# Records of q and k: computed in turned layout and assembled through HBM, in a two-layer attention kernel

## The chip, the cores and the metric

One core of one Trainium2 chip. The metric is the device time of one execution in microseconds; three executions of the kernel before are shown, and the smaller the better. Names used below: PE is TensorE (the matmul engine), DVE is VectorE, ACT is ScalarE, POOL is GpSimd, SP is SyncE, which here only issues transfers (DMAs). SBUF is the on-chip memory of 128 partitions, PSUM the eight accumulation banks that matmuls write, HBM the memory off the core.

## The reference

Two batches of 1024 tokens, 512 wide. Four steps in a row, each added to its input:

```python
x = x + attn_a(layernorm(x), w_qkv_a, w_o_a)   # rope on even/odd pairs, theta 10000
x = x + ffn(layernorm(x), kernel, scale)       # scale * (x @ (2*kernel - 1))
x = x + attn_b(layernorm(x), w_qkv_b, w_o_b)   # rope on halves, base 500000
x = x + ffn(layernorm(x), kernel, scale)
# attention: 32 query heads, 8 key/value heads, 16 wide, causal
q, k, v = split(x @ w_qkv, [512, 128, 128])
q, k = rope(q), rope(k)
scores = q @ k.T / 4 + causal mask;  out = softmax(scores) @ v;  return out @ w_o
```

## The kernel before

It runs four rounds (two batches times two layers), all unrolled inside a loop over `b` and `l`. Each engine has its own queue and works through it in the order in which it is written; semaphores order the engines among each other.

**Stage A** of a round makes q, k and v for 8 tiles of 128 tokens, in slots: in slot n tile n is projected while older tiles are worked on. `PE_SLOT`, `ACT_SLOT` and `DVE_SLOT` list what an engine does in a slot, and `LAG` says for which tile. For a tile, `qkv` (L483) multiplies with the tokens as the stationary operand and 512 or 256 columns of the weights moving, in three products (high times high, high times low, low times high) for precision. ACT copies the result out (`QC`, L747 to L749), DVE and POOL rotate it with tables (`rope_cos` L942, `rope_sin` L1111, `rope` L950). Then each 16-wide head is split in three bf16 parts h, m and l: `part_h` (ACT, L759 and L760), `rest` (POOL, L1122 and L1123), `part_m` (ACT, L766 and L767), `part_l` (DVE, L957 and L959). They are written side by side as a **record** of 7 slots of 16 values (h h h m m l l for q, in another order for k), so that one matmul of depth 112 gives a score of nearly fp32 precision; three more rows hold the negated row maximum of each query. The record is token by token, so PE turns it, head by head, with a matmul against a bf16 identity (`turn_rec`, L532: five batches of eight heads for each tile), and ACT and DVE copy the turned batches from PSUM into `qT` and `kT` (L740, L935).

In the same slots PE and DVE work off the 22 **units** of key/value group 0 (L549 and L551; `unit`, L974): a unit computes scores of a query tile against all its keys and takes their maximum. Units of query tiles 0 to 3 are numbers 0 to 5, those of tiles 4 to 7 are numbers 6 to 21, 16 of them.

**Groups**: then, for each of the 8 key/value groups, scores (L571), exp (ACT, L793), masks (POOL), times v (L589), and the maxima of the next group. The first matmul of L571 in a round is where stage A ends. The `Tail` projects with w_o, adds the FFN and normalises for the next round; ACT and POOL split the next `w_qkv` there (L727, L1098).

SP's queue in a round: the maxima's rows of group 0 (`put_nm`, L409), w_o, 15 more rows, the next w_qkv, and in the last layer of a batch stores and loads of x.

Of the kernel before, what the change touches and what calls it, by code (L numbers as in the profile page):

```python
# [13 lines left out]
P = 128  # L14
# [27 lines left out]
SLOTS = 8  # L42
MAXROW = (SLOTS - 1) * HD
DEPTH = MAXROW + 3
RECS = 3

AHEAD = TILES // 2  # L50
# [9 lines left out]
TURNS = TILES + len(CD_TILES)  # L60
# [136 lines left out]
LAG = {"TX": -1, "Q": 0, "R": 3, "U": 4, "HI": -1, "LO": -1, "QC": 0, "COS": 1, "ROPE": 1, "PH": 1, "PM": 2, "PL": 2,  # L197
       "RC": 3, "ST": -4, "RS": -3, "AP": -2}
# [3 lines left out]
SLOTS_A = range(-4, TILES + 4)  # L202
SLOT_NM = TILES + 2


def slot_work(text, n):

    out = []
    for what, *arg in words(text):
        t = n - LAG[what]  # L210
        if what in ("ST", "RS", "AP"):
            if t % 2 == 0 and 1 <= t // 2 < PAIRS:
                out.append((what, arg, t // 2))
        elif 0 <= t < TILES and (what != "U" or arg[0] < len(units_of(t))):
            out.append((what, arg, t))
    return out


def qkv_bank(t):

    return 2 if t == 1 else 0


def unit_pair(g_is_first, n):


    return n % 2 if not g_is_first or UNITS[n][0] > QT_PER_CHUNK else 1
# [13 lines left out]
def build(nc, x, w_qkv, w_o, w_ffn, scale, cos, sin, eye, tri, out):  # L241
    with ExitStack() as ctx:
# [40 lines left out]
        k_rec = sb("k_rec", [P, RECS, KV, SLOTS, HD], BF16)  # L283
# [175 lines left out]
        def _(pe):  # L459
# [27 lines left out]
            def round_(b, l, r):  # L487
# [7 lines left out]
                def qkv(t, k, part):  # L495

                    T = r * TILES + t
                    if part == 0:
# [5 lines left out]
                        if t == 0:  # L504
                            pe.wait_ge(wq_hi_done, r * KC + KC)
# [742 lines left out]
```

## Time and profile before

| what | us |
|---|---|
| median of 3 executions (1553.36 to 1553.91) | 1553.46 |
| span of the profiled execution, first to last instruction | 1552.2 |
| so what lies around the span, against the median | 1.3 |
| PE busy | 1439.5 (93%) |
| DVE busy | 1132.0 (73%) |
| ACT busy | 998.2 (64%) |
| POOL busy | 413.6 (27%) |
| stage A of the four rounds, from the first matmul of L483 to the first of L571 | 87.05, 83.80, 83.90, 83.33 |

The page gives busy time as a share of the whole span; a stage is read with the view that gives busy times for a stretch. A time such as "x8" in a row covers eight instructions together.

### The profile page before, as it was taken

How to read it: one execution, taken by the hardware profiler on the slowest of the kernel's cores; microseconds unless marked ns; L12 is line 12 of the kernel's file. 1: busy time of each engine (PE TensorE's matmuls, PEld its weight loads, DVE VectorE, ACT ScalarE, POOL GpSimd, SP SyncE). 2: the span in 40 equal slices, each digit the busy share in tenths (PEclk: the TensorE clock that was granted, in tenths of full speed). 3: DMA queues.
4: the chain of work that ended last, by engine and by line, in shares of the span. 5: the costliest groups of instructions: out<-in, count | busy, mean ns of one | idle time of the engine just before them, and what ended most of it. 6: DMA issues, size and time to landing. Idle time of an engine off the chain costs nothing.

```text
span 1552.2 us, 36760 instructions
## 1 busy us (share of the span) xinstructions
PE 1439.5 (93%) x10756; PEld 799.7 (52%) x10756; DVE 1132.0 (73%) x1620; ACT 998.2 (64%) x1800; POOL 413.6 (27%) x786
## 2 busy tenths in 40 slices
PE   5989999998798999999879899999988899999997
PEld 4844444446674444444667444444466744444455
DVE  6897777736788777773768877777377887777646
ACT  4967667663496667675349667766625966776652
POOL 3423222212242322221224222222123422222211
PEclk9999999999899999999989999999998999999999
DMA  3000000001000000000210000000010000000001
GB/s 112 2 29 3 1 1 1 1 1 42 3 1 29 2 1 1 1 1 1 83 69 1 29 3 1 1 1 1 2 41 3 1 30 2 1 1 1 1 21 75
DMA packets 11421, 23.26 MB, mean 15 GB/s; under 512 B 816, under 2 KB 2608, under 8 KB 11312
## 3 DMA queue, kind: packets, MB, share of 16 engines
q1 hardware_dynamic: 11312, 21.89, 4.0%
q8 instruction: 58, 0.95, 0.2%
q14 instruction: 51, 0.42, 0.1%
HBM read 16.91 MB, written 4.19 MB: 14 GB/s over the span
## 4 chain that ended last, share of the span: by engine, by line
PE 73%; DVE 11%; issue 8%; POOL 3%; ACT 3%; DMA 1%; DVEq 0%; POOLq 0%; ACTq 0%; SPq 0%
PE psE L571 17%; PE psO L589 17%; PE psM L549 14%; PE psM L483 13%; DVE mx L974 4%; PE psM L551 3%; PE psT L466 2%; PE psT L532 2%; PE psO L532 2%; ACT probs L793 1%; PE psT L559 1%; DVE stats L876 1%; PE psE L466 1%; PE psM L466 1%; DVE xn L896 1%
## 5 line engine op out<-in xcount | busy, mean ns | idle before, releaser
L974 DVE TENSOR_REDUCE mx<-psM 128x1 f32<-128x768 f32 (+6 forms) x704 | 697.2, 1023 | 189.7 <-PE psM L551 186.7
L793 ACT ACTIVATE probs<-psE 128x512 f32<-128x512 f32 (+1 forms) x1216 | 656.8, 574 | 272.3 <-PE psE L571 261.0
L571 PE MATMUL psE<-qT,kT 115*128 (+4 forms) x1536 | 415.7, 331 | 10.5 <-ACT probs L793 7.4
L549 PE MATMUL psM<-kT,qT 112*128 (+4 forms) x1536 | 376.4, 327 | 17.9 <-DVE mx L974 13.8
L1163 POOL TENSOR_SCALAR_AFFINE_SELECT probs<-probs 128x512 f32<-128x512 f32 x256 | 162.3, 636 | 660.7 <-ACT probs L793 659.9
L589 PE MATMUL psO<-probs,v_grp 128*32 128x512 f32 (+3 forms) x3072 | 323.0, 499 | 6.3 <-POOL probs L1163 3.8
L571 PEld LDWEIGHTS psE<-qT,kT 115*128 (+1 forms) x1536 | 126.2, 97 | 289.0 <-ACT probs L793 152.5
L551 PE MATMUL psM<-tri_b,ident_b 128*128 128x128 bf16 x1024 | 210.3, 220 | 0.0
L549 PEld LDWEIGHTS psM<-kT,qT 112*128 (+1 forms) x1536 | 139.4, 98 | 108.6 <-DVE mx L974 31.1
L551 PEld LDWEIGHTS psM<-tri_b,ident_b 128*128 128x128 bf16 x1024 | 99.7, 97 | 65.5 <-issue 0.6
L589 PEld LDWEIGHTS psO<-probs,v_grp 128*32 128x32 f32 x3072 | 63.3, 108 | 104.3 <-issue 66.7
L483 PE MATMUL psM<-w_lo,xT_hi 128*128 128x512 f32 (+1 forms) x384 | 95.5, 371 | 2.0 <-DVE w_lo L924 2.0
L734 ACT ACTIVATE xT_hi<-psM 128x512 fp32r<-128x512 f32 x64 | 38.0, 601 | 81.0 <-PE psM L466 68.6
L803 ACT ACTIVATE k_rec<-psO 128x512 f32<-128x512 f32 x64 | 38.1, 595 | 70.8 <-PE psO L589 70.8
L1111 POOL TENSOR_TENSOR attn<-attn,sin_s 128x320 f32<-128x320 f32 x64 | 64.7, 1032 | 70.6 <-ACT attn L748 70.6
L1122 POOL TENSOR_TENSOR attn<-attn,probs 128x512 f32<-128x512 f32 x32 | 37.2, 1162 | 137.6 <-ACT k_rec L760 137.6
L483 PEld LDWEIGHTS psM<-w_lo,xT_hi 128*128 128x128 f32 x384 | 66.0, 194 | 12.8 <-DVE w_lo L924 2.8
L483 PE MATMUL psM<-wq_hi,xT_hi 128*128 128x512 f32 (+1 forms) x256 | 65.4, 380 | 3.1 <-ACT wq_hi L727 3.1
L532 PE MATMUL psT<-ident_b,probs 128*128 128x128 bf16 x512 | 42.1, 229 | 20.3 <-DVE k_rec L959 20.3
L740 ACT ACTIVATE qT<-psT 128x1024 bf16<-128x1024 bf16 x48 | 49.0, 1020 | 13.8 <-PE psT L532 13.4
L759 ACT ACTIVATE probs<-attn 128x1536 bf16<-128x1536 f32 x32 | 47.5, 1485 | 16.0 <-DVE attn L950 15.6
L915 DVE TENSOR_TENSOR xT_lo<-psM,xT_hi 128x512 fp32r<-128x512 f32 x64 | 43.3, 687 | 19.5 <-ACT xT_hi L734 17.8
(90 smaller groups left out, 1553.8 us busy)
## 6 DMA issues: line engine op xcount, KB each, us to landing
probs<-in_w_qkv SPq DMA_DIRECT2D x5, 1536.0 KB, 6.3
xs<-in_x SPq DMA_DIRECT2D x8, 512.0 KB, 3.8
attn<-in_w_o SPq DMA_DIRECT2D x4, 1024.0 KB, 5.0
out_x<-xs SPq DMA_DIRECT2D x8, 512.0 KB, 3.0
qT<-nm_rows SPq DMA_DIRECT2D x64, 12.0 KB
probs<-in_w_ffn SPq DMA_DIRECT2D x1, 256.0 KB, 8.1
cos_s<-in_cos SPq DMA_DIRECT2D x1, 128.0 KB, 8.1
sin_s<-in_sin SPq DMA_DIRECT2D x1, 128.0 KB, 8.0
```

The source lines that it names most:

```text
L466: ins = pe.transpose(dst[:, c * P:(c + 1) * P], src[:, c * P:(c + 1) * P], ident[:])
L483: ins = pe.matmul(dst, xT[:, k, c, :], w[:, c, n0:n1], start=first and i == 0, stop=last and i == len(some) - 1)
L532: ins = pe.transpose(bank[:, h * P:(h + 1) * P], src.rearrange("p s d -> p (s d)"), ident_b[:])
L549: ins = pe.matmul(banks[:, at + k0:at + k1], qT[0:MAXROW, g * REP + h, qt * P:(qt + 1) * P], kT[0:MAXROW, g, k0:k1], start=True, stop=not ...
L551: ins = pe.matmul(banks[:, at + keys - P:at + keys], ident_b[:], tri_b[:], start=False, stop=True)
L571: ins = pe.matmul(psE[:, n % 2, at * w:(at + 1) * w], kT[0:DEPTH, g, kb * P:(kb + 1) * P], qT[0:DEPTH, g * REP + j, q0:q0 + w], start=True ...
L589: ins = pe.matmul(psO[VW * j:VW * (j + 1), off:off + w], v_grp[:, kb, :], probs[:, s % PSLOTS, j, 0:w], start=(kb == 0), stop=(kb == (c + ...
L740: act.activation(qT[:, 8 * q:8 * q + 8, t * P:(t + 1) * P], rec_banks[(t + q) % 2].rearrange("p (h n) -> p h n", h=8), ACT.Copy).then_inc( ...
L793: act.activation(probs[:, s % PSLOTS, heads[0]:heads[0] + len(heads), 0:w], psE[:, n % 2, 0:w * len(heads)].rearrange("p (h q) -> p h q", ...
L974: dve.tensor_reduce(mx[:, qt, heads[0]:heads[0] + len(heads)], src, AX.X, ALU.max).then_inc(unit_used.sem, 1)
L1111: ins = pool.tensor_tensor(t4[:, :, a, :], x4[:, :, 1 - a, :], sn[:, :, a * HALF:(a + 1) * HALF].to_broadcast([P, HEADS + KV, HALF]), ALU. ...
L1163: pool.affine_select(out=d, in_=d, compare_op=ALU.is_ge, fill=0.0, base=0, pattern=[[0, REP], [1, P]], channel_multiplier=-1).then_inc(mas ...
```

## The change

The weights become the stationary operand, so q and k come out of PSUM already turned: 128 rows are one of the 16 dimensions of 8 heads each, and the columns are 256 tokens, a pair of tiles. The host reorders the weight columns (`columns`) for this. A **combo** is two blocks of 128 outputs for a pair of tiles, 24 matmuls of 256 columns; block 0 is k, blocks 1 to 4 are q, the sixth is v. Three combos make a pair of tiles, 12 a round. For each combo ACT copies the two halves of the partitions crosswise (`swap`), DVE multiplies by cos, POOL by sin, DVE adds; the parts h, m and l are made by ACT, POOL, ACT and POOL. v is turned back by PE (`v_turn`). The 320 turns of records and their 40 copies of a round are gone, and with them the copies that repeat parts in a record.

The record is now assembled by transfers. For each combo SP writes the three parts to a scratch `rec` in HBM (`put_parts`, 3 DMAs). For every second pair of tiles, which completes 512 tokens, SP waits for these three to land and then reads each block back, seven times, each time into the 16 partitions of a slot (`get_block`, 7 DMAs of 128 KB). So SP issues 36 writes and 70 reads more in a round, in this order of the queue. The `H` of combo n waits until the three writes of combo n-3 have landed, since they share a buffer.

Of the 22 units of group 0, 6 now stand behind combos 9 to 11 and the 16 others behind the last combo; the first of these 16 waits for the blocks 0 and 1 of tokens 512 to 1023, the first scores of group 0 for all blocks. The split of the next w_qkv moves later in the tail, since `wo_hi` now uses the memory of `wq_hi`; the tables are loaded once per round (2 DMAs of 512 KB); DVE fills 32 partitions of `kT` with ones at the start.

SP's queue, before: the start of a round, from the loop's branch to the first maxima of the loop over groups (names are destination and source).

```order
L415 ISA
L409 DMA qT<-nm_rows 3x4x512
L375 REGISTER_ALU
L420 ISA
L420 DMA attn<-in_w_o 128x4x512
L408 REGISTER_ALU
L409 DMA qT<-nm_rows 3x4x512
```

SP's queue, after: the last three combos of a round (9, 10, 11) and what follows them.

```order
L422 DMA rec<-probs 128x2x256 x3
L382 ISA
L429 DMA kT<-rec 16x4096 x7
L429 DMA qT<-rec 16x4096 x7
L417 REGISTER_ALU
L422 DMA rec<-probs 128x2x256 x3
L429 DMA qT<-rec 16x4096 x14
L417 REGISTER_ALU
L422 DMA rec<-probs 128x256 x3
L429 DMA qT<-rec 16x4096 x7
L443 ISA
L444 DMA qT<-nm_rows 3x4x512
```

Ahead of the first maxima of a round there was nothing in the queue; now 106 DMAs stand there, of which these are the last 44.

PE's queue, before: a part of one slot of stage A, with batches of record turns between the parts of a projection.

```order
L483 MATMUL psM<-wq_hi,xT_hi 128x512 x4
L528 REGISTER_ALU
L532 MATMUL psO<-ident_b,probs 128x128 x8
L526 REGISTER_ALU
L532 MATMUL psT<-ident_b,probs 128x128 x8
L483 MATMUL psM<-w_lo,xT_hi 128x512 x4
L483 MATMUL psM<-wq_hi,xT_lo 128x512 x4
L526 REGISTER_ALU
L532 MATMUL psT<-ident_b,k_rec 128x128 x8
```

PE's queue, after: two combos and the turn of v between them.

```order
L547 MATMUL psO<-xT_hi,wq_hi 128x256 x4
L547 MATMUL psO<-xT_hi,w_lo 128x256 x4
L547 MATMUL psO<-xT_lo,wq_hi 128x256 x4
L554 REGISTER_ALU
L557 MATMUL psM<-ident,v_T 128x128 x2
L539 REGISTER_ALU
L547 MATMUL psT<-xT_hi,wq_hi 128x256 x4
L547 MATMUL psT<-xT_hi,w_lo 128x256 x4
```

No record is turned on PE any more, and no unit stands between combos 0 to 8.

```diff
-SLOTS = 8
-MAXROW = (SLOTS - 1) * HD
+SLOTS = 7
+MAXROW = SLOTS * HD
...
+PW = 2 * P
+BLOCKS = 1 + HEADS // KV
+COMBOS = (BLOCKS + 1) // 2
+NP = PAIRS * COMBOS
+Q_PARTS = (0, 0, 0, 1, 1, 2, 2)
+K_PARTS = (2, 0, 1, 0, 1, 0, 1)
+NPARTS = 3
+BUFS = 3
...
-PE_SLOT = "R.0 TX U.0 R.1 Q.0 U.1 R.2 U.2 R.3 Q.1 Q.2 R.4 U.3 Q.3"
-ACT_SLOT = "HI RC.1 PM RC.2 RS RC.3 PH QC"
-DVE_SLOT = "AP RC.0 U.0 COS LO U.1 ROPE U.2 PL RC.4 ST U.3"
+PE_A = slots_a([("Q", 0, None), ("VT", 1, 2), ("TX", 0, 1)])
+ACT_A = slots_a([("RS", 0, 0), ("SW", 0, None), ("M", 2, None), ("H", 1, None), ("VS", 1, 2), ("HI", 0, 1)])
+DVE_A = slots_a([("COS", 0, None), ("AP", 0, 0), ("LO", 0, 1), ("ADD", 0, None), ("ST", 0, 2)])
+POOL_A = slots_a([("SIN", 0, None), ("R1", 1, None), ("L", 2, None)])
+UNITS_AFTER = {9: 2, 10: 2, 11: 2}
...
+            def put_parts(r, n):
+
+                sp.wait_ge(l_ready.sem, l_ready.after(r * NP + n))
+                c, at = n // COMBOS // 2, n // COMBOS % 2 * PW
+                blocks = blocks_of(n)
+                for part in range(NPARTS):
+                    dst = rec[c, part, blocks[0]:blocks[0] + len(blocks), :, at:at + PW].rearrange("b r n -> r b n")
+                    sp.dma_start(dst, parts[:, n % BUFS, part, 0:len(blocks), :]).then_inc(rec_out[n % BUFS], 16)
+
+            def get_block(c, b):
+
+                for slot, part in enumerate(Q_PARTS if b else K_PARTS):
+                    to = slice(slot * HD, (slot + 1) * HD)
+                    dst = qT[to, c, (b - 1) * 8:b * 8, :] if b else kT[to, c, :, :]
+                    sp.dma_start(dst.rearrange("p h n -> p (h n)"),
+                                 rec[c, part, b].rearrange("(d j) n -> d (j n)", d=HD)).then_inc(rec_in[c][b], 16)
+
+            def records(r):
+                for n in range(NP):
+                    put_parts(r, n)
+                    c, second, x = n // COMBOS // 2, n // COMBOS % 2, n % COMBOS
+                    if second:
+                        wait_alone(sp, rec_out[n % BUFS], (r * (NP // BUFS) + n // BUFS + 1) * (16 * NPARTS) + 16)
+                        for b in blocks_of(n):
+                            get_block(c, b)
...
+                    for half in range(2):
+                        at = (2 * x + half) * P
+                        some = products(wq_hi, w_lo)
+                        for i, (xT, w, c) in enumerate(some):
+                            ins = pe.matmul(combo_banks[x][:, half * PW:(half + 1) * PW], w[:, c, at:at + P],
+                                            xT[:, c, p % 2 * 2:p % 2 * 2 + 2, :].rearrange("p a n -> p (a n)"),
+                                            start=i == 0, stop=i == len(some) - 1)
+                    ins.then_inc(combo_done.sem, 1)
...
+                    if first and n in (0, UNITS_0):
+                        for b in range(2):
+                            pe.wait_ge(rec_in[0 if n == 0 else 1][b], r * (16 * SLOTS) + 16 * SLOTS)
...
+                    act.activation(qs[0:P // 2, n % 2, 0:nb, :], bank[P // 2:P], ACT.Copy)
+                    act.activation(qs[P // 2:P, n % 2, 0:nb, :], bank[0:P // 2], ACT.Copy).then_inc(swapped.sem, 1)
...
+                    act.wait_ge(rec_out[n % BUFS], (r * (NP // BUFS) + n // BUFS) * (16 * NPARTS) + 16)
+                    act.wait_ge(rope_ready.sem, rope_ready.after(r * NP + n))
+                    act.activation(parts[:, n % BUFS, 0, 0:nb, :], r_s[:, n % 2, 0:nb, :], ACT.Copy).then_inc(h_ready.sem, 1)
```

## Rows read from the trace of the kernel before

**Rows 1.** The page: its span, busy engines and the chain that ended last.

```profile
span 1552.2 us, 36760 instructions
PE 1439.5 (93%) x10756; PEld 799.7 (52%) x10756; DVE 1132.0 (73%) x1620; ACT 998.2 (64%) x1800; POOL 413.6 (27%) x786
...
PE 73%; DVE 11%; issue 8%; POOL 3%; ACT 3%; DMA 1%; DVEq 0%; POOLq 0%; ACTq 0%; SPq 0%
```

**Rows 2.** Busy time in stage A of four rounds; last, granted clock, DMA share, GB/s.

```profile
13.93:100.98 87.05, 73.42 (x621) 58.82 (x621) 74.33 (x115) 61.20 (x93) 33.45 (x41) 0.96 0.06 24
400.12:483.92 83.80, 72.67 (x624) 58.29 (x622) 71.09 (x110) 61.09 (x93) 29.93 (x37) 0.93 0.04 14
785.06:868.96 83.90, 72.36 (x624) 58.33 (x622) 69.85 (x110) 61.20 (x93) 29.91 (x37) 0.94 0.06 22
1168.03:1251.36 83.33, 72.21 (x624) 58.23 (x622) 70.63 (x110) 61.10 (x93) 29.89 (x37) 0.94 0.04 14
```

**Rows 3.** Groups of instructions by form in stage A of round 2 (785.06 to 868.96).

```profile
L740 ACT ACTIVATE qT<-psT 128x1024 bf16<-128x1024 bf16 x12 | 12.2, 1020 | 3.5 <-PE psT L532 3.5
L759 ACT ACTIVATE probs<-attn 128x1536 bf16<-128x1536 f32 x8 | 11.9, 1485 | 3.6 <-DVE attn L950 3.5
...
L1122 POOL TENSOR_TENSOR attn<-attn,probs 128x512 f32<-128x512 f32 x8 | 9.3, 1163 | 34.7 <-ACT k_rec L760 34.7
...
L747 ACT ACTIVATE attn<-psM 128x512 f32<-128x512 f32 x8 | 4.7, 594 | 3.0 <-PE psM L483 2.9
...
L935 DVE COPY qT<-psT 128x1024 bf16<-128x1024 bf16 x4 | 2.8, 688 | 1.9 <-PE psT L532 1.7 <-DVE var_eps L881 0.2
...
L974 DVE TENSOR_REDUCE mx<-psM 128x1 f32<-128x896 f32 x4 | 4.1, 1069 | 0.0
```

**Rows 4.** PE in order of time: start, duration, instruction.

```profile
794.69 0.64 PE L483 MATMUL psM<-w_lo,xT_hi 128*128 128x256 f32 x4
795.17 0.64 PE L483 MATMUL psM<-wq_hi,xT_lo 128*128 128x256 f32 x4
795.64 0.60 PE L466 MATMUL psE<-ident,xn 128*128 128x128 f32 x4
```

**Rows 5.** SP's issues in order of time: start, time of the issue.

```profile
1.65 0.46 SPq L437 DMA_DIRECT2D ident<-in_eye  x1
2.15 0.43 SPq L396 DMA_DIRECT2D probs<-in_w_qkv  x1
2.63 0.51 SPq L400 DMA_DIRECT2D probs<-in_w_ffn  x1
...
860.96 0.83 SPq L409 DMA_DIRECT2D qT<-nm_rows  x1
862.15 0.41 SPq L420 DMA_DIRECT2D attn<-in_w_o  x1
```

**Rows 6.** The page's DMA issues: KB each, median us from issue to landing.

```profile
probs<-in_w_qkv SPq DMA_DIRECT2D x5, 1536.0 KB, 6.3
xs<-in_x SPq DMA_DIRECT2D x8, 512.0 KB, 3.8
...
out_x<-xs SPq DMA_DIRECT2D x8, 512.0 KB, 3.0
```

**Rows 7.** Windows on a w_o load and on 12 KB of maxima; last, share, GB/s.

```profile
863.23:866.74 3.51, 2.52 (x25) 1.32 (x22) 3.51 (x5) 1.06 (x2) 0.00 (x0) 1.00 0.79 299
...
490.42:490.62 0.20, 0.20 (x5) 0.03 (x2) 0.20 (x1) 0.00 (x0) 0.20 (x1) 1.00 0.18 62
```

**Rows 8.** DVE at the program's start, in order of time.

```profile
1.68 0.16 DVE L859 MEMSET v_grp<- 128x120 f32 x1
...
4.76 1.28 DVE L876 BATCH_NORM_STATS2 stats<-xs 128x6 f32<-128x512 f32 x2 [2.92 <-DMA xs<-in_x]
...
12.44 5.55 DVE L924 TENSOR_TENSOR w_lo<-probs,wq_hi 128x768 fp32r<-128x768 f32 x3 [1.08 <-ACT wq_hi L727]
```

**Rows 9.** POOL's split of w_qkv in a tail; PE after a pause.

```profile
761.19 7.21 POOL L1098 TENSOR_TENSOR w_lo<-probs,wq_hi 128x768 fp32r<-128x768 f32 x4 [19.98 <-PE psM L483]
...
399.72 0.65 PE L466 MATMUL psE<-ident,xn 128*128 128x128 f32 x4 [2.85 <-issue]
400.12 1.84 PE L483 MATMUL psM<-wq_hi,xT_hi 128*128 128x512 f32 x4
```

More of the change, by code:

```diff
@@ L459, in _ @@
         def _(pe):
-            for s in (nm_turned, turned, projected, rec_turned, pv_done, o_turned):
+            for s in (nm_turned, turned, projected, v_turned, pv_done, o_turned):
                 pe.sem_inc(s.sem, s.credit)
@@ L473, in turn_xn, with products @@
                 turn(xn[:, k, :], psE[:, k, :], turned)
-            def products(k, his, los, n0, n1):
-                return [(xT_hi, w, c, n0, n1) for w in (his, los) if w is not None for c in range(KC)] + [
-                    (xT_lo, his, c, n0, n1) for c in range(KC)]
+            def products(his, los):
+                return [(xT_hi, w, c) for w in (his, los) if w is not None for c in range(KC)] + [
+                    (xT_lo, his, c) for c in range(KC)]
             def multiply(k, dst, some, first, last):
-                for i, (xT, w, c, n0, n1) in enumerate(some):
-                    ins = pe.matmul(dst, xT[:, k, c, :], w[:, c, n0:n1], start=first and i == 0,
+                for i, (xT, w, c) in enumerate(some):
+                    ins = pe.matmul(dst, xT[:, c, 2 + k, :], w[:, c, 0:DIM], start=first and i == 0,
                                     stop=last and i == len(some) - 1)
@@ new lines, in part_m @@
+                def part_m(n):
+                    nb = len(blocks_of(n))
+                    act.wait_ge(r1_ready.sem, r1_ready.after(r * NP + n))
+                    act.activation(parts[:, n % BUFS, 1, 0:nb, :], t_s[:, n % BUFS, 0:nb, :], ACT.Copy).then_inc(m_ready.sem, 1)
+                for what, n in ACT_A:
+                    if what == "SW":
+                        swap(n)
+                    elif what == "H":
+                        part_h(n)
+                    elif what == "M":
+                        part_m(n)
+                    elif what == "HI" and 0 <= n < PAIRS - 1:
+                        hi_a(2 * n + 2)
+                        hi_a(2 * n + 3)
+                    elif what == "RS" and 0 <= n < PAIRS - 1:
+                        first_rstd(r * (2 * PAIRS) + n + 1, n + 1)
+                    elif what == "VS" and 0 <= n < PAIRS:
+                        v_copy(n)
@@ L1137, in nm_parts_of @@
+                for what, n in POOL_A:
+                    if what == "SIN":
+                        rope_sin(n)
+                    elif what == "R1":
+                        rest(n)
+                    elif what == "L":
+                        part_l(n)
                 def nm_parts_of(g, c):
@@ L1173, in group @@
                     u = r * KV + g
+                    if first:
+                        wait_alone(pool, vs_ready.sem, vs_ready.after(r * PAIRS + PAIRS - 1))
                     wait_alone(pool, pv_done.sem, pv_done.after(u * NS - 1))
```

470 lines of the change are left out of this document (222 added, 248 removed).

## The prediction

> **What bounds the kernel now.** I read the page first: PE is busy 93% of 1552.2 us and carries 73% of the chain that ended last, DVE 11% [rows 1]. The change leaves the attention groups alone, so the next view is busy time by stretch, over stage A of each round: 87.05 us in round 0 and 83.80, 83.90 and 83.33 us (mean 83.7) in the others [rows 2]. The reader is to see that PE is busy 72 to 73 us of it and DVE 70 to 74, ACT 61, POOL 30: PE and DVE share the bound, and the DMA engines are nearly idle, at 4 to 6%. The groups by form in this stage [rows 3] then say what a turned record costs, and SP's issues and the windows on transfers [rows 5 to 7] what it would cost by DMA. All the difference must come out of four stages of 84 us, and a little of the tail and the start.
>
> **What is removed.** Per round 24 copies of 1.02 us on ACT and 16 of 0.69 us on DVE [rows 3], 24 and 11 us; 320 turns of 128 columns on PE, each no longer than a 256-column matmul, of which four start every 0.48 us [rows 4], so at most 38 us; and the repeated parts on ACT (1.49 us for 1536 columns [rows 3], now 512). If nothing took their place this would be a large gain: PE is left with 12 combos of six times 0.48 us, 2.85 us each [rows 4], or 34 us.
>
> **What is added on the engines.** A combo goes through nine steps on three engines. By the rows: two copies from PSUM of 0.59 us on ACT; on POOL three operations of 1.16 us; on DVE two of about 0.7, the price of a 1024-column bf16 copy being 0.69, which I take as a bound for 512 columns of fp32; two ACT copies of a third of 1.49 us plus a fixed part, 0.6 us [rows 3]. POOL, which was 36% busy, becomes the slowest engine at 3.5 us a full combo and some 0.1 us of handshake on each operation. The queues let a record cross three iterations (sin in n, rest in n+1, l in n+2), and the normalisation, turns and splits of the next pair stand between, some 7 us of DVE and ACT in three combos. I take 4.6 us an iteration (bounds: 3.6, POOL alone, and 6, if the normalisation fully adds). Then L of combo 3 is done 2.85 + 6 x 4.6 = 30.5 us after the first matmul, and L of combo 9, if no transfer held it, after 2.85 + 12 x 4.6 = 58 us.
>
> Behind combo 11 come 16 units which DVE reduces at 1.07 us each [rows 3], 17 us that formerly lay between the projections. So even with free transfers the stage is about 58 + 3.5 (writes) + 7 (the first blocks) + 17 = 86 us. The relief of PE has no place to show: what it did in parallel with DVE now stands in a row.
>
> **What is added on SP.** It issues 106 DMAs a round, in order. An issue takes 0.43 to 0.51 us for loads between 64 KB and 1536 KB, and they start 0.49 us apart [rows 5]; size does not show in it. I take 0.49. A write of three parts then takes 1.5 us to issue, and landing follows 2.0 us later: a 512 KB store lands in 3.0 us [rows 6] and these hold at most 128 KB. So a put-and-wait costs 3.5 us, three of them in a half (512 tokens) 10.5.
>
> **The price of a read.** One moves 128 KB into 16 partitions. No row has that; the bounds are these. Below: from the w_qkv and x loads, (6.3 - 3.8) us for 1024 KB [rows 6], 0.31 us for 128 KB, and then the issue of 0.49 us limits. Above: all these loads go into 128 partitions; if the rate went by the partitions reached, 128 KB into 16 costs like 1024 KB into 128, 2.5 us. The one transfer into few partitions is that of the maxima, 12 KB into 3: 62 GB/s at a share of 0.18, so 3 of 16 engines with 21 GB/s each, against 299/(16 x 0.79) = 24 GB/s each in the w_o load [rows 7]. It shows no slowing, but it is a burst of 4 KB per engine with nothing behind it, where the reads bring 35 times 8 KB per engine. It speaks for the low end; it does not reach the case. I take the middle by ratio between 0.49 and 2.5, **1.12 us**.
>
> The Trainium skill has a rule against this change here: "SBUF — State Buffer", section "Door 1: The DMA port swizzle", says that partitions 0 to 15 are reached through 4 of 16 ports, and gives 104 GB/s for a 1 MiB transfer into them. By that a read would cost 1.26 us. The row of the maxima does not agree, at 62 GB/s into what the page counts as one port.
>
> **The chain that then sets stage A.** SP reads nothing before combo 3. From there SP and the DMA rings are one queue:
> - 30.5 us: L of combo 3.
> - first half: 10.5 + 35 x 1.12 = 49.7.
> - then 9 us: the writes of combo 6 stand behind these reads. ACT's H of combo 9 waits for their landing (3.5), and behind this H on ACT's queue stands everything else of the combos 10 and 11, for which POOL and DVE wait. H, rest, M and L follow with 0.6 + 1.2 + 0.6 + 1.2, and 2 for what is queued between.
> - second half: 49.7.
> - 2.5 us: the last landing, and the maxima's rows, which SP issues (0.83 us [rows 5]) only behind all reads.
>
> Sum 141.4 us against 83.7. The 16 units start at about 30.5 + 49.7 + 9 + 3.5 + 14 x 1.12 + 1.5 = 110 and end at 128, hidden under the reads. In rounds 1 to 3 that is 3 x 57.7 = 173 us.
>
> **Round 0.** The first combo needs all of w_lo, which DVE ends at 12.44 + 5.55 = 18 us, and before that DVE fills 8192 columns of kT. No row has this; 120 columns took 0.16 us [rows 8], so between nothing (if it ends before x lands at 4.76) and 8192/120 x 0.16 = 11 us. With a fixed part taken off (0.06) it is about 7 us, from 1.8 to 9, which pushes what started at 4.76 by 4.4: first combo at 22.5. Stage A then ends at 22.5 + 141.4 = 164 instead of 101: 63 us.
>
> **Other terms.** After a pause PE ran four matmuls in 1.84 us [rows 9], about half of its pace; now it is idle before each round's scores: 1.5 us each, 6. The later split of w_qkv on POOL (7.2 us, ended at 768.4, next stage at 785 [rows 2, 9]) moves by about 8 us and has 16; if that cover were gone, each us late is one us per round. The w_o load stands 50 us later in SP's queue but right behind the maxima's rows, as before: nothing.
>
> Against the profiled 1552.2 us and the 1.3 us around it: 1553.5 + 173 + 63 + 6 = **1796 us**.
>
> **Rivals.**
> 1. The reads run at the rate of their bytes, as the burst of maxima suggests [rows 7], and SP's issue is the bound: a half costs 10.5 + 35 x 0.49 = 27.7, the stage 30.5 + 27.7 + 9 + 27.7 + 2.5 = 97.4. That is 13.7 x 3 + (22.5 + 97.4 - 101) + 4 = 64: **1617 us**. For it: the only row with few partitions. Against it: its size.
> 2. Reads into 16 partitions sustain only a quarter of the engines' rate, 4 x 24 = 95 GB/s [rows 7], and reads of different slots do not overlap: 1.38 us each, a half 58.8, the stage 159.6, so 76 x 3 + 81 + 8 = 317: **1870 us**. For it, in these rows: nothing; against it: 62 GB/s into only 3 partitions. The page named above is the rule with this outcome; by its 1.26 us the sum would be 1835 us.
> 3. The other side: faster. The reads overlap freely and issues of 16-row transfers are short, at or below 0.3 us, so that the writes of combos 4 to 8 never hold an H; and an iteration is POOL's 3.7 us. L of combo 9 at 47, the units' blocks 8 us later, 16 units of 1.07 and 2.5 at the end: 75 us. That is 3 x 8.7 = 26 us, and 22.5 + 75 - 101 = -3.5 in round 0: **1524 us**. It decides where iteration and issue both reach these values; SP's rows, alike for 64 and 1536 KB [rows 5], speak against it.
> 4. No change: free transfers with the iteration as taken, the 86 us above. That is 3 x 2.3 and 22.5 + 86 - 101 = 7.5 in round 0: **1568 us**, still slower by 0.9%; within 0.2% only between this and rival 3.
>
> **How the numbers follow.** Reads between 0.7 and 1.3 us (the forecast's case, 1660 to 1840): 0.50. Rival 1 and reads up to 0.7: 0.28. Rival 2 or slower: 0.15. Rival 3: 0.03, rival 4 and no change: 0.04, of which half is still slower. 1605 to 1850 holds the forecast's case, most of rival 1 and the lower part of rival 2's neighbourhood, 0.8. Faster by over 0.2% (what these runs can tell from no change): 0.03; within: 0.02; slower: 0.95.
>
> **What would show it.** In the profile after: SP's issues of L429 start 1.1 us apart, or the DMA rings lag behind them; GB/s about 115 during the reads; PE idle before the first L571 and released by a DMA into qT; ACT's H (L811) of combos 7, 8 and 9 waiting for DMA; POOL's three groups at 1.16 us. Rival 1 shows reads 0.49 us apart and some 265 GB/s. The prediction is wrong if the sum's form is: if the reads of different slots overlap while others are slow, if an iteration is far from 4.6 us, or if the slow DVE operations beside a busy POOL move the pace from SP to DVE.

## The result and the profile after

| what | before | after |
|---|---|---|
| median of the executions (lowest to highest) | 1553.68 (1553.36 to 1555.03), 4 | 1767.03 (1765.69 to 1771.98), 4 |
| span of the profiled execution | 1552.2 | 1764.0 |
| stage A of the four rounds | 87.05, 83.80, 83.90, 83.33 | 131.50, 132.36, 133.84, 133.12 |

The changed kernel is slower: ratio 1.1375, 95% interval 1.1356 to 1.1394. The spans differ by 211.8 us. The page of the changed kernel first, to be read against [rows 1]: PE has lost 6 us of work and 12 points of its share, and the chain now names transfers and SP's queue.

```profile
span 1764.0 us, 35379 instructions
PE 1433.9 (81%) x9896; PEld 794.0 (45%) x9896; DVE 1088.9 (62%) x1526; ACT 885.9 (50%) x1705; POOL 440.6 (25%) x790
...
PE 59%; DMA 11%; SPq 8%; issue 8%; DVE 7%; ACT 3%; POOL 3%; DVEq 0%; POOLq 0%; ACTq 0%
```

Its windows over the four stages A, the counterpart of [rows 2] (columns as there: PE, PEld, DVE, ACT, POOL busy, granted clock, DMA share, GB/s):

```profile
24.32:155.82 131.50, 68.31 (x405) 55.07 (x405) 57.67 (x87) 32.28 (x68) 39.18 (x47) 0.69 0.63 104
457.20:589.56 132.36, 69.78 (x405) 55.57 (x405) 57.75 (x86) 32.27 (x68) 39.21 (x47) 0.67 0.63 103
892.21:1026.05 133.84, 70.06 (x404) 56.30 (x405) 56.85 (x86) 32.38 (x68) 39.01 (x47) 0.68 0.63 106
1328.01:1461.13 133.12, 69.60 (x404) 55.41 (x405) 57.66 (x86) 32.27 (x68) 39.16 (x47) 0.67 0.63 103
```

All five engines are idle for about half of the stage or longer. ACT's work is down from 61 to 32 us, and nothing came of it. The difference of 211.8 us adds up from these rows: the stages are longer by 44.5, 48.6, 49.9 and 49.8 us (192.8), the first of them starts 10.4 us later (24.32 instead of 13.93), and what lies between a stage's end and the next one's start has grown by 2.2, 1.5, 2.9 and 2.0 us (8.6).

Where a stage's time goes is seen in round 1, whose first matmul is at 457.20. SP's issues (start, time of the issues, count; the 12 writes at 533.79 are those of the combos 6 to 9, with waits between them):

```profile
494.92 1.42 SPq L422 DMA_DIRECT2D rec<-probs  x3
497.85 3.11 SPq L429 DMA_DIRECT2D kT<-rec  x7
501.00 3.20 SPq L429 DMA_DIRECT2D qT<-rec  x7
504.31 1.44 SPq L422 DMA_DIRECT2D rec<-probs  x3
514.59 7.06 SPq L429 DMA_DIRECT2D qT<-rec  x14
521.78 1.32 SPq L422 DMA_DIRECT2D rec<-probs  x3
530.56 3.11 SPq L429 DMA_DIRECT2D qT<-rec  x7
533.79 13.73 SPq L422 DMA_DIRECT2D rec<-probs  x12
549.03 3.11 SPq L429 DMA_DIRECT2D kT<-rec  x7
552.18 3.19 SPq L429 DMA_DIRECT2D qT<-rec  x7
```

A read is issued in 0.44 to 0.5 us, but the issues don't set the pace. The writes issued at 504.31 stand behind 14 reads in the rings (the DMA engines' own queues), and the next reads can go only at 514.59, when they have landed. POOL's two L that bracket the first half (combo 3 and combo 9), and ACT's H of the combos 7, 8 and 9:

```profile
493.72 1.18 POOL L1167 TENSOR_TENSOR probs<-attn,probs 128x512 bf16<-128x512 f32 x1
...
544.74 1.33 POOL L1167 TENSOR_TENSOR probs<-attn,probs 128x512 bf16<-128x512 f32 x1
```

```profile
514.53 0.63 ACT L811 ACTIVATE probs<-attn 128x512 bf16<-128x512 f32 x1 [5.61 <-DMA rec<-probs]
530.51 0.42 ACT L811 ACTIVATE probs<-attn 128x256 bf16<-128x256 f32 x1 [13.35 <-DMA rec<-probs]
540.12 0.63 ACT L811 ACTIVATE probs<-attn 128x512 bf16<-128x512 f32 x1 [7.26 <-DMA rec<-probs]
```

And PE, which waits twice for blocks and once for the maxima's rows behind them:

```profile
513.95 0.29 PE L583 MATMUL psM<-kT,qT 112*128 112x128 bf16 x1 [4.06 <-DMA qT<-rec]
565.13 0.69 PE L583 MATMUL psM<-kT,qT 112*128 112x512 bf16 x2 [13.23 <-DMA qT<-rec]
589.56 1.03 PE L605 MATMUL psE<-qT,kT 115*128 115x512 bf16 x2 [7.84 <-DMA qT<-nm_rows]
```

So, counted from the first matmul: L of combo 3 is done at 37.7 us, H of combo 9 starts at 82.9, its L ends at 88.9, and the first scores start at 132.4. Two windows in which nearly only reads move give their price (the last 2 us of each also hold the three writes that SP issued behind the reads):

```profile
516.00:530.00 14.00, 6.75 (x38) 6.11 (x38) 3.21 (x4) 1.01 (x2) 2.86 (x3) 0.62 0.99 136
567.00:580.00 13.00, 11.49 (x38) 3.54 (x37) 11.74 (x13) 0.00 (x0) 0.00 (x0) 0.50 1.00 146
```

The DMA engines are busy all the time (0.99, 1.00) and move 136 and 146 GB/s, where the w_o load moved 299 at a share of 0.79 [rows 7]. 131,072 bytes at these rates are 0.96 and 0.90 us a read; I use 0.93. Up to the first packet of the writes, 516 to 528 and 567 to 578, the rates are 142 and 153 GB/s, 0.92 and 0.86 us.

### The profile page after: what moved, and what is told of

The parts are those of the page before. It is cut to its first block, busy times and chain, and to the rows that moved or that the text cites. A ratio compares the mean times of both kernels' runs of the same rounds, so it can differ in the third digit from the quotient of the medians.

```text
span 1764.0 us, 35379 instructions
## 1 busy us (share of the span) xinstructions
PE 1433.9 (81%) x9896; PEld 794.0 (45%) x9896; DVE 1088.9 (62%) x1526; ACT 885.9 (50%) x1705; POOL 440.6 (25%) x790
## 4 chain that ended last, share of the span: by engine, by line
PE 59%; DMA 11%; SPq 8%; issue 8%; DVE 7%; ACT 3%; POOL 3%; DVEq 0%; POOLq 0%; ACTq 0%
PE psE L605 15%; PE psO L623 15%; PE psM L583 12%; DMA rec<-probs 9%; SPq L429 6%; PE psM L520 6%; PE psM L585 3%; PE psM L547 2%; PE psT L503 2%; DVE mx L1016 1%; ACT probs L842 1%; PE psT L593 1%; SPq L422 1%; PE psO L547 1%; DVE stats L927 1%
## 5 line engine op out<-in xcount | busy, mean ns | idle before, releaser
L583 PE MATMUL psM<-kT,qT 112*128 (+4 forms) x1536 | 408.2, 350 | 150.9 <-DVE mx L1016 83.5
L811 ACT ACTIVATE probs<-attn 128x512 bf16<-128x512 f32 (+1 forms) x48 | 26.4, 551 | 140.7 <-DMA rec<-probs 104.1
L503 PE MATMUL psE<-ident,xn 128*128 128x128 f32 x136 | 29.7, 376 | 75.4 <-DVE xn L947 75.4
L1155 POOL TENSOR_TENSOR attn<-attn,sin_s 128x512 f32<-128x512 f32 (+1 forms) x48 | 52.7, 1097 | 118.9 <-ACT attn L795 115.3
L1161 POOL TENSOR_TENSOR attn<-attn,probs 128x512 f32<-128x512 f32 (+1 forms) x48 | 48.2, 1005 | 126.4 <-ACT probs L811 126.3
L852 ACT ACTIVATE cos_s<-psO 128x512 f32<-128x512 f32 x64 | 38.1, 595 | 70.9 <-PE psO L623 70.9
L1141 POOL TENSOR_TENSOR w_lo<-probs,wq_hi 128x768 fp32r<-128x768 f32 x17 | 30.7, 1827 | 134.7 <-ACT wq_hi L764 134.7
L1193 POOL TENSOR_SCALAR nm<-mx 128x16 f32<-128x16 f32 x64 | 16.1, 252 | 179.5 <-DVE mx L1016 179.5
L503 PEld LDWEIGHTS psE<-ident,xn 128*128 128x128 f32 x136 | 22.4, 194 | 81.1 <-issue 76.9
L947 DVE TENSOR_SCALAR xn<-xs,mv,rstd 128x512 f32<-128x512 f32 x66 | 46.3, 743 | 6.0 <-DVE rstd L941 6.0
```

Source lines behind the costliest of these rows:

```text
L503: ins = pe.transpose(dst[:, c * P:(c + 1) * P], src[:, c * P:(c + 1) * P], ident[:])
L583: ins = pe.matmul(banks[:, at + k0:at + k1], qT[0:MAXROW, qt // QT_PER_CHUNK, g * REP + h, qt % QT_PER_CHUNK * P:(qt % QT_PER_CHUNK + 1) * P],
L1155: pool.tensor_tensor(t_s[:, n % BUFS, 0:nb, :], qs[:, n % 2, 0:nb, :], sn.to_broadcast([P, nb, PW]), ALU.mult).then_inc(sin_ready.sem, 1)
```

## The experiments

Totals marked "one" are of a single execution, the profiled one; since the four executions of the change spread over 6.3 us, differences of a few us between such totals are read from the stages alone. The kernel before took 1552.4 us beside the first four, 1554.2 beside the next four, 1554.9 and 1554.3 beside the rest. "L3", "H9" and "L9" are the end of L of combo 3, the start of H of combo 9 and the end of its L, in us after the first matmul of round 1. The packets' durations are medians of the trace's packet records in stage A of round 1. The edits are shown shortened.

### Where do the reads lose their time: four shapes of one read

All four move the same 35 times 128 KB (or nearly) in a half, with the same number of issues and the same waits. They leave out that the parts come to stand side by side in a record, and POOL clears what no read fills once at the start, which touches round 0 alone; so the stages of rounds 1 to 3 are compared.

```diff
+ # wide_reads: each read into 128 partitions of 1 KB
+ dst = qT[:, c, (b - 1) * 8 + slot, :] if b else kT[:, c, slot, :]
+ sp.dma_start(dst, rec[c, part, b])
+ # short_packets: 16 partitions as in the change, 1020 bytes at a time
+ dst = qT[to, c, (b - 1) * 8:b * 8, 0:510] if b else kT[to, c, :, 0:510]
+ # reads_32, reads_64: 32 (64) partitions of 4 (2) KB
+ to = slice(slot % 4 * 32, (slot % 4 + 1) * 32)
```

> The 70 reads of a round keep count, source and 128 KB each, but each lands in all 128 partitions (1 KB per partition) instead of 16; the records are thereby not put together. GpSimd also clears the part of qT and kT that no read fills, once, at the start (some 5 us in round 0). Theory D, the 16 destination partitions limit a read: packets of 1 KB take about 46 ns each as in the maxima's transfer, a read costs the 0.45 us of its issue instead of 0.95, stage A of rounds 1 to 3 falls from 132 to 133 us by about 2 x 35 x 0.5 = 35 us to about 98, the whole to about 1625. Theory S, the source side (reading the scratch back from HBM) limits: nothing changes, about 0.95 us a read, stage A 132, total 1764 to 1770.

> The reads go into the same 16 partitions, but as eight pieces of 1020 bytes per partition instead of one of 8 KB (two of 512 columns are left out of every piece and cleared once at the start). Theory D, the destination limits: a piece takes about 120 ns, a read still 0.95 us, stage A 132 to 134, total about 1765. Theory P, the large packet is what is slow: pieces take 46 ns, a read costs its issue of 0.45 us, stage A about 98.

> Each read of 128 KB goes into 32 partitions of 4 KB (slot s into partitions 32*(s mod 4)); the records are not put together, half of qT is cleared once at the start (15 to 20 us of GpSimd, hidden at most partly in round 0). Theory D: the rate doubles with the partitions, 0.48 to 0.5 us a read, 4 KB packets about 0.5 us for two; stage A of rounds 1 to 3 about 98 to 101. Theory S: 132.

> Each read of 128 KB goes into 64 partitions of 2 KB (slot s into partitions 64*(s mod 2)); the records are not put together. Two forms of theory D part here. If the rate goes by the number of partitions, a 2 KB packet takes its free 84 ns (half a KB per partition of the 32 case) and the read is bound by its issue. If it goes by ports, as the Trainium skill has it (SBUF - State Buffer, Door 1: 64 partitions reach no more ports than 32), 2 KB packets take about as long per byte as in the run with 32 partitions, some 115 to 125 ns, and stage A is the same as there, about 98 to 101. Theory S: 132.

| kernel | partitions of a read | total, one | stage A, rounds 1 to 3 | L3, H9, L9 | packet |
|---|---|---|---|---|---|
| after | 16 | 1767.0 (median of 4) | 132.4, 133.8, 133.1 | 37.7, 82.9, 88.9 | 8 KB: 973 ns |
| short_packets | 16 | 1779.9 | 136.7, 136.6, 134.1 | 37.2, 85.1, 91.0 | 1020 B: 126 ns |
| reads_32 | 32 | 1674.1 | 107.9, 107.0, 107.7 | 37.8, 68.8, 77.8 | 4 KB: 266 ns |
| reads_64 | 64 | 1699.8 | 114.4, 116.9, 116.0 | 37.7, 73.9, 80.8 | 2 KB: 84 ns |
| wide_reads | 128 | 1663.2 | 106.7, 108.3, 107.2 | 38.1, 67.9, 78.2 | 1 KB: 46 ns |

Windows on stretches in which reads run, of short_packets, reads_32 and wide_reads, one fence each (a share above 1 means that the recorded times of packets overlap):

```profile
524.00:536.00 12.00, 6.45 (x38) 5.81 (x38) 2.55 (x4) 0.00 (x0) 1.61 (x2) 0.67 1.11 136
```

```profile
535.50:542.00 6.50, 5.82 (x22) 1.98 (x21) 5.61 (x8) 0.00 (x0) 0.00 (x0) 0.50 1.02 243
```

```profile
524.00:529.50 5.50, 4.82 (x19) 1.59 (x18) 4.87 (x7) 0.00 (x0) 0.00 (x0) 0.50 0.87 263
```

The last column decides it: 136, 243 and 263 GB/s. Pieces of 1 KB into 128 partitions take 46 ns, nearly the same pieces into 16 take 126 ns, and the total of short_packets is that of the change or a little worse. It is the destination in 16 partitions that costs, not the number or size of the pieces, and not the way back from HBM, which is the same in all of them. Taking that away is worth 104 us, half of the loss; 32 partitions are nearly as good as 128. reads_64 says something else than it was made for: its reads were issued in 0.62 us instead of 0.45 (7 in 4.29 to 4.44 us), so SP set its pace, and it can't tell whether 64 partitions are better than 32. (The reads of short_packets were issued 0.63 to 0.67 us apart, still less than the 0.96 us that a read takes at 136 GB/s.)

So theory D held in kind, but its numbers did not: 98 us a stage were expected of wide_reads and 98 to 101 of reads_32, and 1625 us in all. Both remain at 107 us a stage, 23 above before, and what holds the stage then is the question of the next experiments.

### What is left without the reads

one_read issues one read of a block instead of seven (the other six slots stay zero, so the scores lack them). units_last is one_read with the six units that stood behind combos 9 to 11 moved behind combo 11.

```diff
- for slot, part in enumerate(Q_PARTS if b else K_PARTS):   # seven reads
+ dst = qT[:, c, (b - 1) * 8, :] if b else kT[:, c, 0, :]
+ sp.dma_start(dst, rec[c, 0, b])                           # one
  # units_last in addition
- UNITS_AFTER = {9: 2, 10: 2, 11: 2}
+ UNITS_AFTER = {}
```

> Of the seven reads of a block one is left, into all 128 partitions (10 reads a round instead of 70); the records are not put together, and GpSimd clears qT and kT at the start (20 us, seen in round 0). What stays is the chain on the engines, so this measures the floor that the prediction put at 86 us with 4.6 us an iteration. By the trace after (L of combo 3 ends 37.7 us after the first matmul, a pair of tiles takes 17.1 us) L of combo 9 comes at 72, and stage A takes 72 + 3.5 + 2 + 17.5 = 95 us in rounds 1 to 3, total about 1615. If instead the engines' chain was only slow because of the transfers beside it, 86 us and 1570.

> This is the kernel with one read of seven per block (the other six thirds and zeros are left out, so its output is not the reference's), with the six score units that stand behind combos 9, 10 and 11 moved behind combo 11, ahead of the other 16. Theory A: these six tie PE's next combo to DVE's reduce and so to POOL's sin, which is why L of combo 9 stands at 78.8 us after the first matmul and not at about 70; then L of combo 9 falls to 68 to 73 us, and the stage changes little (99 to 105 us, from 101), because six units now stand behind it. Theory B: the pace is set by the copies, sums and normalisation alone; L of combo 9 stays at 77 to 80 us and the stage grows by six units, to 107 to 113 us.

one_read: 1646.7 us (one), stages 111.6, 101.2, 100.1 and 101.2; L3 37.8, H9 65.3, L9 78.8. units_last: 1625.1 us (one), stages 107.3, 95.9, 96.8 and 95.1; L3 37.6, H9 57.7, L9 65.5. Round 0 of both holds POOL's clearing of qT and kT. one_read was expected at 95 us a stage and 1615 in all; it missed by 6 and 32, since in it PE stood at units in the middle of the combos:

```profile
504.70 0.50 PE L580 MATMUL psM<-kT,qT 112*128 112x384 bf16 x1 [4.89 <-DVE mx L1013]
513.50 0.39 PE L580 MATMUL psM<-kT,qT 112*128 112x512 bf16 x1 [3.36 <-DVE mx L1013]
```

DVE's reduce stands in its queue behind the addition of the same combo, which waits for POOL's sin of it; PE's next combo stands behind the unit. Moved away, that loop is gone, L9 comes 13 us earlier, and the stage gains 5, because six more units now follow in a row. These six are dear, as DVE's rows of units_last show, two of the six and then eight of the other 16:

```profile
499.44 0.96 DVE L1015 TENSOR_REDUCE mx<-psM 128x2 f32<-128x768 f32 x1 [1.13 <-PE psM L582]
501.53 0.96 DVE L1015 TENSOR_REDUCE mx<-psM 128x2 f32<-128x768 f32 x1 [1.13 <-PE psM L582]
...
518.86 9.01 DVE L1015 TENSOR_REDUCE mx<-psM 128x1 f32<-128x896 f32 x8 [0.26 <-PE psM L582]
```

The kernel gives the first six units one pair of PSUM banks (`unit_pair`) and the others two in turn. So PE and DVE alternate on the six, 12.8 us for them (494.86 to 507.63) or 2.1 each, where the others follow each other in 1.1. Theory A's ranges were both missed on the low side, 65.5 for L9 against 68 to 73 and 96 for the stage against 99 to 105; theory B's, 77 to 80 and 107 to 113, lie further off. So even with one seventh of the reads, the engines' order makes the stage 96 us, 12 more than before. No run gave the six units a second pair.

### The front end

stats_early takes the statistics of a pair of tiles one combo earlier and the normalisation ahead of the cos; memset_later moves the fill of kT.

```diff
- DVE_A = slots_a([("COS", 0, None), ("AP", 0, 0), ("LO", 0, 1), ("ADD", 0, None), ("ST", 0, 2)])
+ DVE_A = slots_a([("AP", 0, 0), ("COS", 0, None), ("LO", 0, 1), ("ADD", 0, None), ("ST", 0, 1)])
  # memset_later alone
- dve.memset(kT[96:P], 1.0)      # ahead of the first statistics
+ dve.memset(kT[96:P], 1.0)      # behind the copy of tri_b
```

> Only DVE's order changes: the statistics of the next pair stand in the second iteration of a pair instead of the third, and the normalisation ahead of the product with cos instead of behind it. Theory L: an iteration is long because the normalisation hangs in one loop with turn, combo, swap, sin and sum; then L of combo 3 comes at about 29 us instead of 37.7, the reads still take their 0.95 us each, and stage A falls to about 124, total about 1730. Rival: GpSimd's three operations and the handshakes set an iteration; then L of combo 3 stays at 36 to 38 and the total within 10 us of 1764.

> The changed kernel with one edit: DVE fills the 8192 columns of kT behind the copy of the triangle instead of ahead of the first statistics. If the fill is what holds the first projection, the first matmul moves from 24.3 us to 17 to 19 us, and the total falls by that, to 1759 to 1762 us, the four stages unchanged (131 to 134 us). If the start hangs on something else (x, w_lo), the first matmul stays at 24 us and the total at 1766 to 1768 us.

stats_early: 1748.4 us (one), stages 127.8, 129.1, 128.2, 128.1, L3 33.3 instead of 37.7. PE turns the next pair's tiles (L503), which in the changed kernel came 17.07 us apart, each time after a wait for xn:

```profile
484.19 1.96 PE L503 MATMUL psE<-ident,xn 128*128 128x128 f32 x8 [5.45 <-DVE xn L947]
...
501.26 1.97 PE L503 MATMUL psE<-ident,xn 128*128 128x128 f32 x8 [5.37 <-DVE xn L947]
```

In stats_early they are 14.0 us apart:

```profile
462.96 1.09 PE L503 MATMUL psE<-ident,xn 128*128 128x128 f32 x8 [0.37 <-DVE xn L947]
476.98 1.97 PE L503 MATMUL psE<-ident,xn 128*128 128x128 f32 x8 [3.33 <-DVE xn L947]
```

So the pace up to L3 was the loop of statistics, root, normalisation and turn: 17.07 us for three combos, 5.7 an iteration. The edit gave half of what theory L expected (L3 at 29, the stage at 124, 1730 us); its rival expected L3 to stay at 36 to 38. What it gives at L3 (4.4, 6.7 and 4.9 us in rounds 1 to 3) reappears for the most part in the stage (3.3, 5.6 and 5.0), as it must if SP's queue from L3 on is the bound.

The clock has a part in this loop. In each loop PE is idle until the turn, and then the combo behind the turn runs at a lower granted clock than the two that follow. Two windows of the changed kernel in which PE is busy throughout, the first on that combo:

```profile
485.00:490.00 5.00, 5.00 (x32) 5.00 (x31) 2.72 (x5) 1.60 (x3) 1.80 (x2) 0.68 0.13 39
490.00:495.00 5.00, 5.00 (x44) 5.00 (x44) 2.73 (x7) 2.87 (x8) 3.09 (x3) 1.00 0.01 3
```

Up to L3 the combos 0, 2 and 5 took 4.6, 4.2 and 4.2 us at 0.63 to 0.71 of full clock, the combos 1, 3 and 4 3.0 to 3.1 at 1.00. That is at most 4 us of the 37.7; no run tells the clock from the rest of the loop.

memset_later: 1771.1 us (one), where 5 to 8 below the change's 1767.0 was expected. The first matmul did move, from 24.3 to 18.9 us, but stage A of round 0 grew from 131.5 to 141.0, so that it ended 4.1 us later than in the change; the other three stages are 133.5, 133.3 and 134.3. DVE of this kernel:

```profile
20.75 6.88 DVE L979 MEMSET kT<- 32x8192 bf16 x1 [1.76 <-issue]
27.65 1.29 DVE L926 BATCH_NORM_STATS2 stats<-xs 128x6 f32<-128x512 f32 x2
```

The fill now stands ahead of the statistics of the second pair and of every cos. In the changed kernel these statistics started at 24.37, here at 27.65, and the whole loop with them. The expectation was wrong: the fill has no free place there, it only changes whom it holds. In both places an idle stretch of 1.75 or 1.76 us stands ahead of it, so it costs DVE 8.6 us and not 6.9.

### Other ways to put the records together

full_records writes each part into all slots that hold it (from a source that is repeated, 60 writes a round instead of 36) and reads a block with one transfer into 112 partitions. It computes all that the change does. records_and_order adds stats_early and memset_later to it, records_order_units the six units behind combo 11, and six_buffers doubles the buffers of the parts, so that H of combo n waits for the writes of combo n-6, and SP waits ahead of a block's read for one more group of writes.

```diff
- for slot, part in enumerate(Q_PARTS if b else K_PARTS): ...  # 7 reads into 16 partitions
+ src = parts[:, n % BUFS, part, a:a + 1, :].to_broadcast([P, len(at_slots), PW])
+ sp.dma_start(dst, src).then_inc(rec_out[n % BUFS], 16)      # a write for each block and part, to all its slots
+ dst = qT[0:MAXROW, c, (b - 1) * 8:b * 8, :] if b else kT[0:MAXROW, c, :, :]   # 1 read of 896 KB
  # six_buffers
+ PB = 6      # parts[:, n % PB], rec_out[n % PB]
```

> SP writes each part to all its slots (a source repeated two or three times, 60 writes a round instead of 36, 9.2 MB instead of 3.9), and reads a block with one transfer of 896 KB into 112 partitions (10 reads instead of 70); everything is computed. Theory D: a read takes about 2.4 us as a load of w_o does, no H waits for a write any more, L of combo 9 at 72 to 74, then 6 issues, landing, two reads and 16 units: stage A about 102 to 104, total about 1645. If the scratch itself (HBM, its 512-byte pieces) is the limit, the writes, now 2.3 times as many bytes, keep it at 130 or more.

> Both together: records written out in full and read in one piece, DVE's order as in stats_early; the ones in kT are set after the split of the first weights instead of before the first tile. Theory D and L: L of combo 9 at about 53, stage A about 84 to 90, the start 5 us earlier than in the kernel after, total 1565 to 1600, near the kernel before. If theory L is false, the same as full_records less 5 us.

> The kernel with records written in full, one read of 112 partitions per block, the early statistics and the fill moved, and in addition the six score units moved behind combo 11. Theory A (the six units tie PE to DVE): L of combo 9 from 74.5 to 66 to 70 us, the stages from 107 to 102 to 106, total 1650 to 1665. Theory B: L of combo 9 stays at 73 to 75 us and the stages grow to 113 to 118, total 1690 to 1710.

> The kernel of records_order_units (full records, one read of 112 partitions per block, early statistics, fill moved, six score units behind combo 11) with six buffers of parts instead of three, so that ACT's H of combos 6 to 8 no longer waits for writes that stand behind the first half's reads in SP's queue, and H of combos 9 to 11 waits only for writes of the combos 3 to 5. Theory A: this hold is what keeps L of combo 9 at 74 us when it came at 65.5 us with free reads; then L of combo 9 falls to 59 to 66 us, the stages from 107 to 96 to 101 us, the total from 1664 to 1625 to 1640 us. Theory B: the broadcast writes themselves (10 us of DMA queue per issue burst) pace the second half; L of combo 9 falls but the stage stays at 104 to 108 us, the total at 1650 to 1665. Either way it stays above the kernel before (1554), since the engines' chain with free reads alone was 96 us.

| kernel | total | stage A, rounds 1 to 3 | L3, H9, L9 |
|---|---|---|---|
| full_records | 1689.2, one | 113.9, 113.8, 113.3 | 37.8, 73.7, 81.2 |
| records_and_order | 1667.8; ratio 1.0735 (1.0715 to 1.0755) | 107.0, 108.4, 107.0 | 31.2, 66.6, 74.5 |
| records_order_units | 1663.9, one | 108.0, 106.9, 106.2 | 33.0, 68.2, 74.1 |
| six_buffers | 1646.4; ratio 1.0593 (1.0567 to 1.0618) | 104.6, 101.4, 100.4 | 32.7, 51.2, 59.1 |

The first two missed what I had expected by 44 us and more (1645, and 1565 to 1600). In records_order_units the total is theory A's, the stages lie just above A's 102 to 106, and L9 is theory B's: with H held by writes (ACT waited 6.43 us for one at 503.68), moving the units neither helped nor cost. full_records shows the reason in SP's queue:

```profile
482.24 0.34 SPq L430 DMA_DIRECT2D kT<-rec  x1
482.62 0.42 SPq L430 DMA_DIRECT2D qT<-rec  x1
483.16 4.08 SPq L425 DMA_DIRECT2D rec<-probs  x6
493.28 0.81 SPq L430 DMA_DIRECT2D qT<-rec  x2
```

The issues shrank, but the next reads still start 11 us later. In these 11 us lie two blocks of 896 KB, 7.3 us at the 253 GB/s of this kernel's reads (a window from 494 to 502), and 1792 packets of 512 B, 27 ns each on 16 engines, 3.0 us. For a whole round that makes 36 us for 9.2 MB of reads and 30 for 17,920 packets of writes. six_buffers was made to tell the hold of H from this volume. The hold went: ACT waits for a transfer once more, 1.70 us, and L9 comes at 59.1. The stage gained only 3 to 6 us, because the blocks are now what is late:

```profile
513.38 0.69 PE L586 MATMUL psM<-kT,qT 112*128 112x512 bf16 x2 [11.74 <-DMA qT<-rec]
```

Behind this wait come the 16 units, 17 us. The DMA engines are busy for 0.66 of the stage of 104.6 us, 69 us. 8 of these, the writes of the first combos, lie ahead of L3 at 32.7, and 61 of the 71.9 us behind it (a share of 0.24 and of 0.85): with the volume alone the stage could not end before 94 us, and the rest are gaps in the queue, such as SP's waits for a landing. L9 came out as theory A had it (59 to 66); the stage lies in theory B's range (104 to 108) in round 1, between the two in round 2 and in A's (96 to 101) in round 3, and the total lies between the two ranges, above 1640 and below 1650. That the volume paces the second half, as B had it, is therefore likely and not shown by a run with less volume. No version tried is faster than the kernel before.

## Why the prediction was right

The direction, the mechanism and the range held; the forecast of 1796 us was 29 too high. Against the profiled execution, 1764.0 + 1.7 around it, the terms were:

| term | predicted | measured |
|---|---|---|
| stage A, rounds 1 to 3 | +173 | +148.3 |
| round 0, start and stage | +63 | +54.8 |
| clock after the pauses, and all else between the stages | +6 | +8.6 |

- **L of combo 3 at 30.5 us.** Measured 37.7. The step that failed is the iteration of 4.6 us: up to there it is 5.7, the loop through the normalisation. That is inside the bounds I had put (3.6 to 6), near the end "if the normalisation fully adds", and stats_early shows that this loop matters. From L3 to L9 units_last takes 27.9 us for six combos, 4.65 each, but this agreement is luck: it is the mean of 5.7 for the three combos up to L6 (54.8), with a normalisation among them, and 3.6 for the three after it, without one. There is no common iteration of 4.6; there are both bounds, one after the other. The clock inside stage A, up to 4 us of this term, was put at nothing.
- **The price of a read, 1.12 us.** (The middle by ratio of 0.49 and 2.5 is 1.11; the slip is 0.9 us a stage.) Measured 0.93 at a DMA share of 0.99. Right in kind: wide_reads and short_packets together show that reads into 16 partitions are slow because of where they go, and rival 1 (the rate goes by the bytes, 0.49) falls. The row on which rival 1 stood, 62 GB/s into 3 partitions [rows 7], says nothing of a sustained rate. By the Trainium skill ("SBUF — State Buffer", "Door 1: The DMA port swizzle") it was to be 104 GB/s, 1.26 us; the trace has 136 to 146 GB/s, so the rule points the right way and its number is too low here. Successive reads go to slots that the page puts at different ports; whether they overlap, and whether that makes the difference, no run shows.
- **A put-and-wait of 3.5 us.** The first took 2.9 (494.92 to 497.85). The others are not separate from the reads ahead of them: 504.31 to 514.59 holds 14 of them.
- **The first half and the 9 us behind it.** Predicted 53.2 from L3 to H9 and 5.5 to the end of L9; measured 45.2 and 6.0. The writes of combo 6 behind the reads, and H of combo 9 behind them, were there as described. The 8 us too many are the 35 reads (35 x 0.19 = 6.7) and shorter puts. With L3 7.2 us too early they cancelled: H9 was forecast at 83.7 and came at 82.9. Two errors of opposite sign, so this agreement proves neither.
- **The second half.** Predicted 52.2 with its landing, measured 43.5, again 35 x 0.19 and some. Nothing cancelled it here: 7.5 to 8.9 us in each of four rounds, 34, is the miss of 30 and a little more.
- **Free transfers would leave 86 us.** This was wrong, in a term that did not enter the sum: one_read has 101. The six units behind combos 9 to 11 tie PE to DVE and POOL, which I had not seen in the order, and with them away it is 96. Against 86 that is 7.5 for L9 (65.5 instead of 58, from the late L3) and 3 behind it, where the six units now stand in a row. Rival 4's 1568 us and rival 3's 1524 us are both below the 1625 us of units_last; with this order of the engines neither could come about.
- **Round 0.** The first matmul was forecast at 22.5 and came at 24.3. The fill took 6.88 us, as estimated (7), but it started only at 3.48, and DVE did nothing for the 1.75 us ahead of it, so the first statistics began at 10.39 instead of 4.76, 5.6 us later where 4.4 was forecast:

```profile
3.48 6.88 DVE L910 MEMSET kT<- 32x8192 bf16 x1 [1.75 <-issue]
10.39 0.69 DVE L927 BATCH_NORM_STATS2 stats<-xs 128x6 f32<-128x512 f32 x1
```

- **The clock, 1.5 us a round.** In the 16 us from the first scores on the granted clock was 0.94 before and is 0.86 after, the first row of before, the second of after:

```profile
483.92:500.00 16.08, 15.43 (x125) 7.73 (x123) 13.50 (x16) 12.79 (x25) 4.90 (x13) 0.94 0.01 2
```

```profile
589.56:605.64 16.08, 15.94 (x115) 8.21 (x115) 11.18 (x13) 11.78 (x23) 2.81 (x5) 0.86 0.11 43
```

  0.08 x 16.08 is 1.3 us, and PE got through 10 matmuls fewer. In the first 2.95 us of these stretches the clock was 0.70 before and 0.50, the lower of its two levels (1.2 GHz), after; ahead of them PE had been idle for 7.84 us in the changed kernel. Measured growth is 1.5 to 2.9 a round. The rest I did not test; the tails of the change have one more turn for the next round, before which PE waited 1.80 us for xn at 451.73.
- **What would show it.** L429's issues were to be 1.1 us apart or the rings to lag; they lag. GB/s was to be about 115 during the reads and is 136 to 146. POOL's three operations were to take 1.16 us; over 512 columns the medians are 1.27, 1.17 and 1.15. ACT's H of combos 7, 8 and 9 waits for DMA, as said, and PE before the first scores is released by a DMA into qT, if by the maxima's rows that stand behind the blocks.

**Where the gain went.** PE's turns and 40 copies were taken away, and ACT is idle for three quarters of the stage. The 48.6 us that stage A of round 1 lost lie, by the experiments, in four layers: 25.7 us are the slow destination (132.4 to 106.7 with wide_reads), another 5.5 the other reads (to 101.2 with one_read), 5.3 the place of the six units (to 95.9 with units_last), and the last 12 (to 83.8) what remains of the new order: the loop ahead of combo 3, and 22 units in a row that were once worked beside the projections, six of them at 2.1 us. The layers depend on the order in which they are taken off, and the last is the remainder, not an experiment of its own; stats_early, in which L3 comes 4.4 us earlier, suggests that about 4 of it can be had back once transfers don't set the pace; no run has both. The granted clock, 0.67 to 0.69 in stage A against 0.93 to 0.96 before, runs through all four layers and was not taken apart.

## What to carry to other kernels

When work is moved from engines to transfers, price one transfer by where it lands and how many of its kind follow, not by its bytes: a burst of 12 KB says nothing of 35 transfers of 128 KB. Ask of each wait in a transfer queue what stands ahead of it in the same rings, for a write behind reads takes the reads' time and holds the engine that wants the buffer. And before an idle resource is given work, count what the busy ones did in parallel with what is removed: here the units that had hidden behind the projections remained as a row of their own.

## What was new of the hardware

- Pieces of 1020 B into 16 partitions took 126 ns (the median; 46 at the 10th percentile), pieces of 1 KB into 128 partitions 46 ns. Into 32 partitions the reads ran at 243 GB/s, against 136 to 146 into 16.
- SP issued a read of 128 KB into 64 partitions of 2 KB in 0.62 us, into 16, 32 or 128 partitions in 0.44 to 0.50; into 16 partitions in pieces of 1020 B it took 0.63 to 0.67. No run explains it.
- DVE's small operations beside a busy POOL: the 2-column product took 0.16 us alone and 0.92 us in the loop (L937 in memset_later at 7.21 and 48.85, the latter inside POOL's product from 48.48 to 49.75). They are part of the 17.07 us of the normalisation's loop.
